# Attention's rounds dissolved into three strands, expert sums issued in four pieces, and the first unit of the last quarter taken ahead

## The chip, the core and the metric

One core of a Trainium2 chip runs the whole program. The core has five engines with their own instruction queues: TensorE (PE), VectorE (DVE), ScalarE (ACT), GpSimd (POOL) and SyncE (SP), which here only issues DMAs; GpSimd issues the indirect DMAs (gather and scatter). The metric is the device time of one execution in microseconds, as the median of several runs.

## The reference

The input x has 16 sequences of 512 rows with 256 channels, in fp32. Four layers follow each other, each added to its input after a layer norm:

```
x = x + gated_deltanet(layernorm(x))      # a recurrence over the 512 rows, 16 heads of 16
x = x + moe(layernorm(x))                 # 16 experts, 4 a row, and a shared one
x = x + attention(layernorm(x))           # causal, 16 heads of 16, rmsnorm and rope on q and k
x = x + moe(layernorm(x))                 # the same weights as above

# deltanet, one row t:                     # moe:
S = S + beta * outer(v - S k, k)           scores = sigmoid(x @ gate_w.T)
o = S q                                    idx = top_k(scores + gate_b, 4)
                                           w = 2.5 * scores[idx] / sum(scores[idx])
# attention:                               y = sum_e w_e * (silu(x @ w1_e.T) * (x @ w3_e.T)) @ w2_e.T
p = softmax(q k.T / 4 + causal)            y = y + shared expert
out = (p v) @ Wo
```

## The kernel before

**One list of stages.** `stages()` (line 127) makes one list, `order`, of named stages such as `step`, `w_dot` or `y_sum`, and each engine then walks the whole list and issues what is its own in each stage. So the order on every engine's queue is the order of that list, and an instruction that waits holds all behind it on its engine. The list is woven from generators ("strands"): every `yield` ends a step and gives a cost, `step()` advances a strand by one step, and `run(credit)` advances it while its credit lasts. `misc` is the pool of seven PSUM banks; the eighth, bank 6, collects the product with V.

**Units and groups.** A unit is 512 rows. Units 0 to 15 are the rows of the first moe (unit 4q + n: quarter q of the sequences 4n to 4n + 3), units 16 to 31 those of the second (unit 16 + b: sequence b). A unit has four rows of work J of 128 rows each, J = 4 * unit ... + 3. `GROUPS = [4, 4, 4, 1, 3, 2, 4, 4, 4, 2]` units form groups, which are routed together: three groups cover units 0 to 11, then unit 12 alone, units 13 to 15, 16 and 17, 18 to 21, 22 to 25, 26 to 29, and 30 and 31. For each group the strand `heads()` computes layer norm, gate and shared expert (`head`), the positions (`route`), and scatters each J with four indirect DMAs into an expert-sorted buffer (`x_row`: GpSimd scales the row, `x_move`: four scatters). For J from 64 to 119 it then yields SPACE more times. The strand `tiles()` works through 16 tiles a unit and 16 more a group: 256 KB of weights and 128 KB of rows in, 128 KB out. The strand `sums()` gathers for each J its four expert rows (`y_in`: four indirect DMAs on GpSimd into a ring of five tiles) and accumulates them on VectorE (`y_sum`, line 1371). Routing of a group waits in the list until the sums of the group two before it are in.

**The recurrence.** VectorE runs the 512 steps in four quarters of 128 (`step`, lines 1084 to 1100, in three thirds). After every third `heads` gets the credit HEAD_RATE, `tiles` TILE_RATE, `sums` SUM_RATE and the projection of the next quarter PROJECT_RATE. Operations of a step are tied in a chain: products with k and with q (L1084, L1086), their reductions (L1089, L1092), the difference (L1094), its outer product (L1097), the new state (L1100).

**The turnover.** After the last quarter the state's outputs are transposed (`u_turn`), `first_rows` projects them for units 12 to 15, all four side by side, while tiles and sums step along but heads does not. Then `second_setup` loads the constants of attention by DMA and GpSimd prepares them (lines 1620 to 1632), and only then heads may go on to unit 12. `prepare(0)` advances all strands until the sum of J = 48 is in the list, since sequence 0 needs it.

**Attention.** For each of 16 sequences (batches) `attention(b)` yields turns with a phase: 1 for projection, norm, rope and the split of q and k (32 turns), 2 and 3 for the scores, 4 for the output projection (12 turns). After each turn `tiles` gets PHASE_RATE[phase]; `heads` steps every second turn, `sums` every fourth. The heads form four groups of four. For each group `largest(hg)` issues eleven stages of scores (`m_dot`, L899) with VectorE's row maxima (`m_max`, L1202), then splits the maxima into three bf16 parts, transposes them (`m_part`, `m_turn`, `m_out`). `weigh(hg)` issues for four key tiles of 128 and four heads the scores again with the maximum subtracted by a second matmul (`w_dot`, L916 and L918), the exponential on ScalarE (`w_exp`, L1516), the causal select of the diagonal 128 x 128 on GpSimd (L1650), and the product with V (`w_pv`, L930), which waits for the select and stands about four turns behind its scores; at the end `w_out` copies bank 6. The rounds: round 0 is `largest(0)`, round r has `weigh(r - 1)` beside `largest(r)`, round 4 is `weigh(3)` alone, and a round ends when both are done.

Of the kernel before, what the change touches and what calls it, by code (L numbers as in the profile page):

```python
# [15 lines left out]
NQ = SEQ // 128  # L16
# [100 lines left out]
def stages():  # L117
# [129 lines left out]
    def attention(b, norm):  # L247
# [62 lines left out]
        def largest(hg):  # L310
            k = 4 * b + hg
            pend, l = None, 11 * k
            for qt in range(NQ):
                nh = {0: 4, 1: 2, 2: 1, 3: 1}[qt]
                for h0 in range(4 * hg, 4 * hg + 4, nh):
                    mi, mf = yield from misc.take()
                    put("m_dot", b, qt, h0, nh, mi, mf)
                    if pend:
                        put("m_max", *pend)
                        misc.give(pend[-1], "mx", pend[1] + 1)  # L320
                    pend = (b, l, qt, h0, nh, mi)
                    l += 1
                    yield
            put("m_max", *pend)
            misc.give(pend[-1], "mx", pend[1] + 1)
# [9 lines left out]
            yield  # L335

        def weigh(hg):
            k = 4 * b + hg
            pend = None
            for kt in range(NQ):  # L340
                for a in range(4):
                    w = 16 * k + 4 * kt + a
                    mi, mf = yield from misc.take()
                    put("w_dot", k, kt, a, mi, mf)
                    if pend:
                        put("w_exp", *pend)
                        misc.give(pend[-1], "we", w)
                    pend = (k, kt, a, mi)
                    if a == 3 and kt:
                        put("w_pv", k, kt - 1)  # L350
                    yield
            put("w_exp", *pend)
            misc.give(pend[-1], "we", 16 * k + 16)
# [1489 lines left out]
```

## Time and profile before

| | |
|---|---|
| three runs | 5775.86, 5779.35, 5791.94 us, median 5779.35 |
| profiled execution | 5783.49 us, span 5782.3 us, mean granted TensorE clock 0.799 |
| busy over the span | PE 3420.9 (59%), DVE 4123.7 (71%), ACT 1976.3 (34%), POOL 1764.7 (31%) |
| chain that ended last | DVE 41%, PE 30%, issue 11%, POOL 9%, ACT 4%, DMA 3% |
| HBM | 378.89 MB read, 209.72 MB written, 102 GB/s over the span |

The shares over the whole span are means over stages of different kind, so they say little by themselves; the windows among the rows below give the stages apart. The profiled execution's own time is its span and 1.2 us around it.

### The profile page before, as it was taken

How to read it: one execution, taken by the hardware profiler on the slowest of the kernel's cores; microseconds unless marked ns; L12 is line 12 of the kernel's file. 1: busy time of each engine (PE TensorE's matmuls, PEld its weight loads, DVE VectorE, ACT ScalarE, POOL GpSimd, SP SyncE). 2: the span in 40 equal slices, each digit the busy share in tenths (PEclk: the TensorE clock that was granted, in tenths of full speed). 3: DMA queues.
4: the chain of work that ended last, by engine and by line, in shares of the span. 5: the costliest groups of instructions: out<-in, count | busy, mean ns of one | idle time of the engine just before them, and what ended most of it. 6: DMA issues, size and time to landing. Idle time of an engine off the chain costs nothing.

```text
span 5782.3 us, 71376 instructions
## 1 busy us (share of the span) xinstructions
PE 3420.9 (59%) x20276; PEld 2403.0 (42%) x20372; DVE 4123.7 (71%) x10439; ACT 1976.3 (34%) x4743; POOL 1764.7 (31%) x2760
## 2 busy tenths in 40 slices
PE   6312053663436533263548878876788778877664
PEld 3101031452315422152435555543565555545554
DVE  1999989999899988998356656665566556654333
ACT  3111021231213311031236545644555545544232
POOL 1010014303461133403352233235211433244523
PEclk8655576796668866697779999987999989988887
DMA  1210001462215421363532334311233323333776
GB/s 48 114 40 7 0 20 48 136 173 67 67 57 172 140 64 55 113 189 114 154 110 75 99 121 126 95 54 65 79 90 90 115 89 117 113 99 121 244 226 200
DMA packets 429265, 593.40 MB, mean 103 GB/s; under 512 B 57680, under 2 KB 304080, under 8 KB 428752
## 3 DMA queue, kind: packets, MB, share of 16 engines
q1 hardware_dynamic: 379728, 454.55, 26.3%
q0 software_dynamic: 49152, 134.28, 7.0%
q8 instruction: 173, 2.83, 0.2%
q14 instruction: 212, 1.74, 0.1%
HBM read 378.89 MB, written 209.72 MB: 102 GB/s over the span
## 4 chain that ended last, share of the span: by engine, by line
DVE 41%; PE 30%; issue 11%; POOL 9%; ACT 4%; DMA 3%; SPq 2%; another core or an unknown queue 1%; DVEq 0%; ACTq 0%; POOLq 0%
PE psum L1020 5%; DVE rec L1084 5%; DVE rec L1086 4%; DVE skb L1089 4%; DVE rec L1097 4%; DVE rec L1100 4%; POOL xbuck L1669 4%; DVE region L1092 3%; PE psum L930 3%; PE psum L878 3%; PE psum L1028 3%; DVE psum L1202 2%; DVE acc L1371 2%; POOL yg L1679 2%; PE psum L918 2%
## 5 line engine op out<-in xcount | busy, mean ns | idle before, releaser
L1020 PE MATMUL psum<-xgT,w 128*128 128x128 f32 x5376 | 798.9, 296 | 105.1 <-issue 57.9
L1679 POOL DMA_INDIRECT yg<-ybuck,words x512 | 529.6, 1034 | 988.1 <-issue 641.2
L1020 PEld LDWEIGHTS psum<-xgT,w 128*128 128x128 f32 x5376 | 729.2, 209 | 160.2 <-issue 123.2
L1028 PE MATMUL psum<-w_w2T,hid 128*128 x1344 | 475.0, 438 | 360.1 <-DVE hid L1353 227.0
L1202 DVE CUSTOM_DVE_ANT_0 psum<-psum,xo 128x128 f32<-128x128 f32 (+3 forms) x1024 | 473.7, 520 | 224.5 <-PE psum L899 204.5
L1669 POOL DMA_INDIRECT xbuck<-srow,words x512 | 521.9, 1019 | 152.3 <-issue 128.9
L810 PE MATMUL psum<-w_ident,xn 128*128 128x128 f32 x512 | 105.8, 343 | 773.5 <-ACT xn L1388 767.8
L1516 ACT ACTIVATE region<-psum 128x512 f32<-128x512 f32 (+3 forms) x1024 | 412.0, 443 | 348.4 <-PE psum L918 313.7
L1551 ACT ACTIVATE xgT<-psum 128x256 f32<-128x256 f32 x672 | 257.1, 383 | 760.7 <-PE psum L1010 709.2
L1650 POOL TENSOR_SCALAR_AFFINE_SELECT region<-region 128x128 f32<-128x128 f32 x1024 | 288.8, 300 | 670.5 <-ACT region L1516 656.2
L1038 DVE SCALAR_TENSOR_TENSOR sil<-sil,psum 128x128 f32<-128x128 f32 (+1 forms) x472 | 139.4, 295 | 448.9 <-ACT sil L1560 366.2
L1371 DVE SCALAR_TENSOR_TENSOR acc<-yg,words,acc 128x256 f32<-128x256 f32 x512 | 254.4, 497 | 233.5 <-DMA yg<-ybuck,words 87.4
L810 PEld LDWEIGHTS psum<-w_ident,xn 128*128 128x128 f32 x512 | 73.7, 174 | 803.1 <-ACT xn L1388 746.0
L1028 PEld LDWEIGHTS psum<-w_w2T,hid 128*128 128x128 f32 x1344 | 223.4, 205 | 440.0 <-issue 436.0
L1010 PE MATMUL psum<-w_ident,xg 128*128 128x128 f32 x1344 | 280.1, 294 | 170.3 <-DMA xg<-xbuck 162.6
L1097 DVE TENSOR_TENSOR rec<-ub,region 128x512 f32<-128x512 f32 x512 | 370.8, 724 | 12.5
L1084 DVE TENSOR_TENSOR rec<-rec,region 128x512 f32<-128x512 f32 x512 | 362.3, 708 | 12.5
L1100 DVE TENSOR_TENSOR rec<-rec 128x512 f32<-128x512 f32 x512 | 358.4, 700 | 11.8
L1086 DVE TENSOR_TENSOR rec<-rec,region 128x512 f32<-128x512 f32 x508 | 357.9, 704 | 0.0
L1585 POOL TENSOR_SCALAR small<-small 128x4 f32<-128x4 f32 (+1 forms) x80 | 30.3, 379 | 1060.9 <-DVE small L1051 1058.1
L930 PE MATMUL psum<-region 128*32 128x512 f32 (+3 forms) x2048 | 278.5, 468 | 121.4 <-POOL region L1650 96.9
L1089 DVE TENSOR_REDUCE skb<-rec 128x32 f32<-128x512 f32 x512 | 347.4, 678 | 0.1
(201 smaller groups left out, 7576.4 us busy)
## 6 DMA issues: line engine op xcount, KB each, us to landing
w<-in_w13T SPq DMA_DIRECT2D x672, 256.0 KB
xg<-xbuck SPq DMA_DIRECT2D x672, 128.0 KB
ybuck<-yrow SPq DMA_DIRECT2D x672, 128.0 KB
xbuck<-x SPq DMA_DIRECT2D x40, 512.0 KB, 5.3
x_scratch<-res SPq DMA_DIRECT2D x64, 256.0 KB
acc<-x_scratch SPq DMA_DIRECT2D x128, 128.0 KB
xbuck<-srow,words POOLq DMA_INDIRECT x512
yg<-ybuck,words POOLq DMA_INDIRECT x512
```

Source lines behind the costliest of these rows:

```text
L930: o = e.matmul(psum[32 * a:32 * a + 32, 6, kt * 128:SEQ], vb[:, kt, k % 4 * 4 + a, :], P[w % 8][:, 0:n], start=(kt == 0), stop=(kt == NQ - ...
L1020: o = e.matmul(psum[:, mi, half], w13[I % 3][:, k, half], xgT[I % 2][:, k, :], start=(k == 0), stop=(k == 1), skip_group_check=True)
L1028: o = e.matmul(psum[:, mi, 0:D], hid[hi][:, 0:128], w2T[:, bass.ds(expert.pop(I), 1), :].rearrange("p a b -> p (a b)"), start=True, stop=True)
L1084: e.tensor_tensor(tk[:, :, :, :], S[:, :, :, :], ktt, ALU.mult).then_inc(s["scan"], 1)
L1086: e.tensor_tensor(tq[:, :, :, :], S[:, :, :, :], bc(kq[:, :, t - 1, 16:32], 2, 16), ALU.mult).then_inc(s["scan"], 1)
L1089: e.tensor_reduce(skb[:, :, :], tk[:, :, :, :], AX.X, ALU.add).then_inc(s["scan"], 1)
L1097: e.tensor_tensor(tk[:, :, :, :], bc(ub[:, :, :], 3, 16), ktt, ALU.mult).then_inc(s["scan"], 1)
L1100: e.tensor_tensor(S[:, :, :, :], S[:, :, :, :], tk[:, :, :, :], ALU.add).then_inc(s["scan"], 1)
L1202: o = e.tensor_tensor_reduce(scores, scores, maskw[:, SEQ - n:SEQ], -1.0, BIG, ALU.add, ALU.min, mx[:, qt, h0 + i:h0 + i + 1])
L1516: e.activation(P[w % 8][:, 0:n], psum[:, mi, 0:n], ACT.Exp, scale=HD ** -0.5).then_inc(s["we"], 1)
L1669: e.indirect_dma_start(xbuck[g % 2], bass.IndirectOffsetOnAxis(ap=posu[g % 2][:, J - ROWS0[g], k:k + 1], axis=0), srow[J % 2], None).then_ ...
L1679: e.indirect_dma_start(yg[y % 5], None, ybuck[g % 2][0:TILES_OF[g] * 128, :], bass.IndirectOffsetOnAxis(ap=posu[g % 2][:, J - ROWS0[g], k: ...
```

## The change

The list of stages is woven differently; no arithmetic changes.

- In attention the rounds are gone. One strand issues the maxima of the head groups one after the other (group 2 and 3 wait until the weights of the group two before are issued). When a group's maxima are issued, its small chain (parts, transpose, copy) starts as a strand of its own. One strand issues the weights, each group as soon as its chain is out, and the last V product with its copy becomes a strand of its own. A turn steps all of them and has phase 3 once the first chain is out, before that phase 2.
- `y_sum` is issued as four stages; for J below 48 the strand yields between them. SUM_RATE goes from 0.2 to 0.35.
- SPACE goes from 4 to 2, PHASE_RATE[3] from 0.04 to 0.06.
- After the last quarter the rows of unit 12 go first; then `heads` may start on it while the rows of units 13 to 15 are issued. A head waits in the list for its own unit's rows. GpSimd's preparation of the constants moves behind the scatter of unit 12's group, as `second_fill`.

```diff
-HEAD_RATE, TILE_RATE, SUM_RATE, PROJECT_RATE = 0.6, 0.5, 0.2, 0.15
-SCATTER, SPACE = 1.3, 4
-PHASE_RATE = {LIGHT: 0.32, 1: 0.32, 2: 0.2, 3: 0.04, 4: 0.3}
+HEAD_RATE, TILE_RATE, SUM_RATE, PROJECT_RATE = 0.6, 0.5, 0.35, 0.15
+SCATTER, SPACE = 1.3, 2
+PHASE_RATE = {LIGHT: 0.32, 1: 0.32, 2: 0.2, 3: 0.06, 4: 0.3}
...
-        def largest(hg):
+        turning, closing, out, weighed = [], [], set(), set()
+
+        def largest():
+            for hg in range(4):
+                while hg >= 2 and hg - 2 not in weighed:
+                    yield
...                                   # m_dot and m_max as before
+                turning.append(Strand(turn(hg)))
+
+        def turn(hg):
...                                   # m_part, m_turn, m_out as before
+            out.add(hg)
+
+        def weigh():
+            for hg in range(4):
+                while hg not in out:
+                    yield
...                                   # w_dot, w_exp and three w_pv as before
+                weighed.add(hg)
+                closing.append(Strand(close(hg)))
+
+        def close(hg):
             k = 4 * b + hg
             yield
             yield
             put("w_pv", k, NQ - 1)
             yield
             put("w_out", k)
-        for hg in range(5):
-            both = [Strand(weigh(hg - 1))] if hg else []
-            both += [Strand(largest(hg))] if hg < 4 else []
-            while not all(t.done for t in both):
-                for t in both:
-                    t.step()
-                yield 2 if hg == 0 else 3
+        heads_of, weights = Strand(largest()), Strand(weigh())
+        while not (heads_of.done and weights.done and all(t.done for t in closing)):
+            for t in closing + [weights] + turning + [heads_of]:
+                t.step()
+            yield 3 if out else 2
...                                   # heads()
+                while b < NB and b not in added:
+                    yield LIGHT
                 yield from head(b)
...
             filled.add(g)
+            if UNIT0[g + 1] == NB - 3:
+                put("second_fill")
...                                   # sums()
-                put("y_sum", g, J)
+                for k in range(4):
+                    put("y_sum", g, J, k)
+                    if J < 48 and k < 3:
+                        yield LIGHT
...                                   # after the last quarter
     rows = [Strand(first_rows(NQ - 1, n)) for n in range(4)]
+    while not rows[0].done:
+        for t in rows[0:1] + streams[1:]:
+            t.step()
+    turned.add(NQ - 1)
     while not all(t.done for t in rows):
-        for t in rows + streams[1:]:
+        for t in streams + rows:
             t.step()
     put("second_setup")
-    turned.add(NQ - 1)
```

## Rows read from the trace of the kernel before

**Rows 1.** The page's busy tenths in 40 slices of 144.6 us.
```profile
PE   6312053663436533263548878876788778877664
...
DVE  1999989999899988998356656665566556654333
```

**Rows 2.** Windows: length, busy us of PE, PEld, DVE, ACT, POOL; clock, DMA, GB/s.
```profile
159.00:2699.00 2540.00, 1029.87 (x4902) 738.00 (x4902) 2374.61 (x4692) 503.40 (x1260) 613.77 (x654) 0.70 0.28 86
2699.00:2941.00 242.00, 128.07 (x748) 110.84 (x748) 99.53 (x335) 58.42 (x162) 98.73 (x137) 0.74 0.47 143
2941.00:5305.00 2364.00, 1860.18 (x12622) 1254.89 (x12719) 1454.59 (x4851) 1222.88 (x2803) 821.82 (x1709) 0.90 0.31 95
```

**Rows 3.** Waits of TensorE, 2941 to 5305: us in total, times, longest.
```profile
PE psum L930 <- POOL region L1650: 96.9, 43, 8.1
...
PE psum L916 <- DVE region L1202: 29.3, 23, 8.0
```

**Rows 4.** Windows of batches 5 and 6, L1028 alone (two matmul records a tile).
```profile
3667.00:3796.00 129.00, 13.85 (x42) 6.83 (x42) 0.97 0.31 92
3796.00:3962.00 166.00, 1.88 (x6) 1.06 (x6) 0.79 0.20 64
```

**Rows 5.** Windows of the rounds and the last round: batch 5, then batch 6.
```profile
3735.00:3770.00 35.00, 32.43 (x248) 16.23 (x251) 27.41 (x120) 23.87 (x59) 14.00 (x47) 1.00 0.16 47
3770.00:3784.00 14.00, 13.26 (x114) 7.46 (x113) 1.43 (x7) 10.21 (x31) 5.82 (x21) 1.00 0.13 39
...
3858.00:3918.00 60.00, 39.49 (x250) 17.95 (x252) 41.00 (x167) 22.05 (x50) 33.09 (x62) 0.77 0.22 68
3918.00:3949.00 31.00, 18.92 (x107) 8.38 (x107) 6.65 (x19) 10.22 (x28) 25.92 (x48) 0.86 0.31 100
```

**Rows 6.** Timeline of VectorE in a step with a sum: start, length, operation.
```profile
1433.23 2.25 DVE L1371 SCALAR_TENSOR_TENSOR acc<-yg,words,acc 128x256 f32<-128x256 f32 x4
1435.39 0.69 DVE L1097 TENSOR_TENSOR rec<-ub,region 128x512 f32<-128x512 f32 x1
```

**Rows 7.** Timeline of VectorE in a step without one.
```profile
1445.65 0.68 DVE L1092 TENSOR_REDUCE region<-rec 128x32 f32<-128x512 f32 x1
1446.24 0.18 DVE L1094 TENSOR_TENSOR ub<-region,skb 128x32 f32<-128x32 f32 x1
1446.45 0.69 DVE L1097 TENSOR_TENSOR rec<-ub,region 128x512 f32<-128x512 f32 x1
```

**Rows 8.** Window of the recurrence, L1371 alone: busy us (instructions).
```profile
159.00:2699.00 2540.00, 69.42 (x144) 0.70 0.28 86
```

**Rows 9.** The chain in order of time: the load of batch 0.
```profile
2927.02 3.80 DMA xnT<-x_scratch
```

**Rows 10.** Timeline of GpSimd in the turnover: setup, a gather, first scattered row.
```profile
2741.43 0.19 POOL L1623 CAST w_attn<-w_attn 128x4 bf16<-128x4 f32 x1 [3.06 <-DMA w_attn<-in_sel]
...
2746.29 1.01 POOL L1679 DMA_INDIRECT yg<-ybuck,words  x1 [0.16 <-issue]
...
2793.40 0.78 POOL L1659 TENSOR_SCALAR srow<-x,stq 128x256 f32<-128x256 f32 x1 [5.93 <-DVE words L1336]
```

**Rows 11.** Window of the 32 tiles of unit 12, L1028 alone.
```profile
2833.00:2913.00 80.00, 20.32 (x64) 10.33 (x64) 0.99 0.70 203
```

**Rows 12.** Windows with L1028 alone: no tiles, and the tail.
```profile
3811.00:4116.00 305.00, 0.00 (x0) 0.00 (x0) 0.80 0.19 62
...
5305.00:5568.00 263.00, 59.43 (x168) 28.30 (x168) 0.86 0.77 231
```

**Rows 13.** Timelines of GpSimd and TensorE around a burst of scatters.
```profile
3914.02 1.07 POOL L1669 DMA_INDIRECT xbuck<-srow,words  x1 [0.16 <-issue]
...
3919.15 1.06 POOL L1650 TENSOR_SCALAR_AFFINE_SELECT region<-region 128x128 f32<-128x128 f32 x4
...
3919.51 1.33 PE L930 MATMUL psum<-region 128*32 128x384 f32 x6 [0.44 <-issue]
```

**Rows 14.** Window of the scattered rows of units 18 to 21, L1659 alone.
```profile
3892.00:4080.00 188.00, 9.41 (x16) 0.80 0.18 63
```

More of the change, by code:

```diff
@@ L308, in attention @@
             yield 1
-        def largest(hg):
-            k = 4 * b + hg
[L312 to L325, printed above, removed]
+        turning, closing, out, weighed = [], [], set(), set()
[3 more added lines that the diff above has]
+                    yield
+                k = 4 * b + hg
+                pend, l = None, 11 * k
+                for qt in range(NQ):
+                    nh = {0: 4, 1: 2, 2: 1, 3: 1}[qt]
+                    for h0 in range(4 * hg, 4 * hg + 4, nh):
+                        mi, mf = yield from misc.take()
+                        put("m_dot", b, qt, h0, nh, mi, mf)
+                        if pend:
+                            put("m_max", *pend)
+                            misc.give(pend[-1], "mx", pend[1] + 1)
+                        pend = (b, l, qt, h0, nh, mi)
+                        l += 1
+                        yield
+                put("m_max", *pend)
+                misc.give(pend[-1], "mx", pend[1] + 1)
+                turning.append(Strand(turn(hg)))
+        def turn(hg):
+            k = 4 * b + hg
             for i in range(3):
@@ L335, in largest @@
             yield
-        def weigh(hg):
-            k = 4 * b + hg
[L339 to L353, printed above, removed]
+            out.add(hg)
+        def weigh():
+            for hg in range(4):
+                while hg not in out:
+                    yield
+                k = 4 * b + hg
+                pend = None
+                for kt in range(NQ):
+                    for a in range(4):
+                        w = 16 * k + 4 * kt + a
+                        mi, mf = yield from misc.take()
+                        put("w_dot", k, kt, a, mi, mf)
+                        if pend:
+                            put("w_exp", *pend)
+                            misc.give(pend[-1], "we", w)
+                        pend = (k, kt, a, mi)
+                        if a == 3 and kt:
+                            put("w_pv", k, kt - 1)
+                        yield
+                put("w_exp", *pend)
+                misc.give(pend[-1], "we", 16 * k + 16)
+                weighed.add(hg)
+                closing.append(Strand(close(hg)))
+        def close(hg):
+            k = 4 * b + hg
             yield
@@ L1361, in vector @@
             elif name == "y_sum":
-                g, J = u
-                a, j = acc[J % 2], J - ROWS0[g]
+                g, J, k = u
+                a, j, y = acc[J % 2], J - ROWS0[g], 4 * J + k
                 dv.wait_ge(s[f"ai{J % 2}"], 16 * (J // 2) + 16)
                 dv.wait_ge(s["rv"], RV0[g + 1])
-                for k in range(4):
-                    y = 4 * J + k
-                    dv.wait_ge(s[f"yg{y % 5}"], 16 * (y // 5) + 16)
-                    if k:
-                        dv.wait_ge(s["ysum"], y)
-                    e.scalar_tensor_tensor(a, yg[y % 5], ck[g % 2][:, j, k:k + 1], a, ALU.mult,
-                                           ALU.add).then_inc(s["ysum"], 1)
+                dv.wait_ge(s[f"yg{y % 5}"], 16 * (y // 5) + 16)
+                if k:
+                    dv.wait_ge(s["ysum"], y)
+                e.scalar_tensor_tensor(a, yg[y % 5], ck[g % 2][:, j, k:k + 1], a, ALU.mult,
+                                       ALU.add).then_inc(s["ysum"], 1)
     def scalar():
@@ L1619, in gpsimd @@
                 e.tensor_tensor(xo[oi], xo[oi], boA[:, :], ALU.add).then_inc(s["rb"], 1)
-            elif name == "second_setup":
+            elif name == "second_fill":
                 po.wait_ge(s["oadd"], 64)
@@ L1774, in sync @@
             elif name == "y_sum":
-                g, J = u
-                sp.wait_ge(s["ysum"], 4 * J + 4)
-                e.dma_start(of_half(J, out_rows), acc[J % 2]).then_inc(s[f"ao{J % 2}"], 16)
+                g, J, k = u
+                if k == 3:
+                    sp.wait_ge(s["ysum"], 4 * J + 4)
+                    e.dma_start(of_half(J, out_rows), acc[J % 2]).then_inc(s[f"ao{J % 2}"], 16)
             elif name == "end":
```

## The prediction

> **What bounds the kernel now.** First the busy tenths, to see that the run has two halves: in slices 2 to 19 of 40 VectorE stands at 8 or 9 tenths, in slices 22 to 37 TensorE at 6 to 8 [rows 1]. Windows put numbers to them [rows 2]: the recurrence, 159 to 2699 us (VectorE busy 2375 of 2540); a turnover, 2699 to 2941, in which no engine is over 53% busy; attention, 2941 to 5305 (TensorE 1860 of 2364, DMA share 0.31). Then comes a tail to the end of the span, 5782, whose first 263 us move 231 GB/s at DMA share 0.77 [rows 12]. Then the waits of TensorE within attention: the longest is the product with V waiting for GpSimd's causal select, 97 us in 43 waits, and 29 us go to banks that VectorE's maxima hold [rows 3]. Last, a batch without row traffic beside one with it: 129 us with 21 tiles against 166 with 3 [rows 4], and their phases, where the difference lies [rows 5].
>
> **The change part by part.**
>
> *Sums in four stages.* In the recurrence the four accumulations of a row are one block, 2.16 us from its start to the start of the next multiply (1433.23 to 1435.39), 0.54 each [rows 6], since each waits for the one before. Step operations without such a tie start 0.59 apart for 0.68 of work, so they overlap by 0.09; a tied pair (ub, then the multiply by it) starts 0.21 apart for 0.18, so it doesn't [rows 7]. A piece put between a tied pair fills such a place. Apart, I take a piece at 0.45 instead of 0.54, which gives 0.36 a row, and another 0.14 for tied pairs that were empty: 0.5 a row. The recurrence has 144 accumulations, 36 rows [rows 8]: 18 us off, on the engine that sets the end there. Bounds: 0 (each piece keeps 0.54) and 36 x 0.9 = 32 (0.40 a piece, and three tied pairs each 0.1 better). The pace stays: 4 steps of the strand at rate 0.2 and 7 at 0.35 both give a row in 7 thirds of a step.
>
> The Trainium skill (VectorE: DVE Perf Modes, "The DRAIN you can't avoid") speaks against this: a chain of operations with a semaphore after each took as long there as one with a single semaphore at the end. By it these 18 us would be 0. The trace does not agree as far as it goes: tied operations start later after their predecessor's end than untied ones, by 0.12 us [rows 7]. It stands below as a rival.
>
> *The turnover.* Unit 12 gates it: its first rows, head, routing, 4 scattered rows, 32 tiles and first sum, after which batch 0's load ends the chain's wait at 2931 [rows 9]. Today the rows of all four units go first, then the setup, for whose constants GpSimd waits 3.1 us and on which it then works until its next gather, 2741.4 to 2746.3 [rows 10]. From there to unit 12's first scattered row, 2793.4, GpSimd's queue holds 28 gathers of sums, 1.3 us apart [rows 10]. Three gains: the setup leaves the chain, 8 us; three quarters of the row work no longer stand ahead of the head, though they still share the engines with it, 10 us; and a row of sums takes 7 steps of its strand instead of 4, so that some 10 gathers fewer precede the scatter, 12 us. Late next is the tile pass: the sums put off run beside it, some 8 rows of 0.79 MB (six transfers of 128 KB), 6 MB on top of the 16 MB that its 80 us at 203 GB/s move [rows 11]. Were 231 GB/s [rows 12] the ceiling, it would last 17 us longer; I take 5. So 25 us off; bounds 0 and 50.
>
> *Attention without rounds.* Counted in the loops: today 18 turns of maxima alone, then four rounds of 20, 98 of the 143 turns of a batch. New: the maxima of groups 0 and 1 run on (turns 1 to 22), group 0's weights start at 20, group 1's at 36 with group 2's maxima, group 2's at 55, group 3's at 71, and the last close ends at 91: 136 turns a batch. The instructions are the same. In the quiet batch TensorE is busy 32.4 of 35 us in the rounds and 13.3 of 14 in the last one [rows 5]: at most some 4 us can go, and 1.2 more tiles (0.06 x 73 turns for 0.04 x 80) want half of it. In the busy batch the same phases take 91 us, 58.4 of them busy [rows 5]. There a select sits behind a burst of four scatters, 3914.0 to 3919.15, and the product that needs it starts at 3919.51 [rows 13]. What changes is the last product of a group: three turns of the next group's dots now stand ahead of it in TensorE's queue, so that they are issued while it would wait; behind it the bank of the sum is copied by ScalarE, and the next group's first product, four turns later, waits for that copy. The other three products have the lead they had. Of the 97 + 29 us [rows 3] I count a quarter, that product's share, as gone: 31. Six come back: of a batch's turns some 42 now have weights without maxima (31 before), in which a lead of four turns is shorter. 25 us off over 16 batches. Bounds: 90 off (most of the 126) and 40 on.
>
> *Two pauses for four.* A scattered row of units 16 to 29 takes 12 turns now (row, move, four pauses, the strand stepping every second turn) and 8 then. 16 rows lie within 188 us [rows 14]; they would take 125. The bursts are as many as before; that they come closer can make GpSimd the bound, and is the slow rival.
>
> *Earlier groups, higher rate.* No tile runs from 3811 to 4116 [rows 12], since units 18 to 21 are scattered only by 4080 [rows 14]. They would be ready 62 us sooner, and a batch takes 22 tiles, not 21. Carried through the turns: that group ends in batch 11, units 22 to 25 end in the middle of batch 15, and units 26 to 29 are scattered by turn 100 of it instead of 120, so that some 4 of their tiles, beside the 4 left over today, and 5 rows of sums get in before attention ends. I count 8 tiles (0.52 MB: weights 256 KB, in and out 128 KB each) and 5 rows of sums out of the tail: 8.1 MB, at 231 GB/s 35 us, 36 with a shorter restart. In attention the 8 tiles cost 25 us at most, at the tail's pace of 84 tiles in 263 us [rows 12]; half or more fall where TensorE idles: 10 on. Bounds of the tail: 0 and 60 off.
>
> **Sum.** -18 - 25 - 25 + 10 - 36 = -94. The profiled execution took 5783.5 us (span 5782.3); the median of the runs, 5779.35, is 4 lower. 5783.5 - 94 - 4 = 5685.
>
> **Rivals.**
> 1. Attention and tail give nothing: the added tiles cost in attention what they save behind it, and the stalls only move. For: TensorE is 79% busy there. Against: 33 us of the busy batch's 91 are idle [rows 5]. Then 18 + 25 off: 5736.
> 2. Slower: GpSimd becomes the bound of attention. Its burst with the scaled row is 5.6 us, and 8 turns hold 8 selects of 0.3: 8.0 us of work, in turns of weights alone that last 14 us for 20 [rows 5], 5.6 for 8. If each of the 56 closer rows costs 2.5 us more than today, 140 are added: 5825. It decides from 94 / 56 = 1.7 us a row. For: the 97 us of waits for the select. Against: a row costs GpSimd the same work as now, and 12 turns at 0.7 us are hardly longer than it even today.
> 3. Both kinds of stall go (the bound of 90): 5620.
> 4. The four stages save nothing, the rest holds, as the skill's rule would have it: 5703.
> 5. The last large group does not come forward: forced advances and the wait for the sums two groups back keep it behind 5305. Then +10 and -36 fall away: 5711.
>
> **Chances.** Forecast 0.42, rival 1 0.20, rival 2 0.14, rival 3 0.12, rivals 4 and 5 0.06 each. About 0.3%, 17 us, is what a measurement can tell from no change. Rival 2 lies above that, a third of rival 1, with its own spread, within it: faster 0.79, same 0.07, slower 0.14. The range for 8 in 10 leaves out most of rival 2 and the lower part of rival 3: 5600 to 5780. The forecast's own is 5640 to 5725.
>
> **What would show it.** Right: the accumulations of the recurrence singly among step operations, and its stretch some 18 us shorter; unit 12's first scattered row within 60 us of the recurrence's end, and batch 0 some 25 us earlier; tiles of units 26 to 29 before attention ends; the wait of the V product for the select under 80 us; a tail near 440. Wrong: attention as long as its 2364 us, the select's wait above 100 us (then rival 2), or a turnover that keeps its 242 us.

## The result and the profile after

Four executions of the changed kernel took 5710.86 to 5734.44 us, median 5720.71; four of the kernel before on the same chip 5773.94 to 5791.94, median 5777.60. The ratio is 0.9894 [0.9874, 0.9914]: 1.1% faster, 57 us by the medians, where 94 were forecast. The time lies within the range (5600 to 5780) and just inside the forecast's own (5640 to 5725). The profiled execution took 5734.44 us, the slowest of its four; that of the kernel before took 5783.49.

The page of the changed kernel (span; busy us of each engine; busy tenths in 40 slices), against [rows 1]:

```profile
span 5733.2 us, 71459 instructions
PE 3423.1 (60%) x20279; PEld 2404.4 (42%) x20372; DVE 4101.4 (72%) x10439; ACT 1958.1 (34%) x4743; POOL 1769.6 (31%) x2760
PE   6312054573536634163558878875888787877664
DVE  1999988999899988998456646665667466745333
```

The work is the same and the outline too. The windows of the three stretches of [rows 2], and the tail:

```profile
159.00:2683.00 2524.00, 1041.46 (x4902) 746.90 (x4902) 2359.31 (x4691) 504.06 (x1260) 617.40 (x653) 0.70 0.28 87
2683.00:2917.00 234.00, 122.45 (x748) 106.72 (x748) 97.50 (x336) 57.75 (x162) 97.90 (x136) 0.75 0.50 149
2917.00:5272.00 2355.00, 1868.02 (x12714) 1259.87 (x12808) 1463.19 (x4894) 1211.23 (x2820) 841.36 (x1728) 0.90 0.32 98
5272.00:5733.00 461.00, 285.58 (x1597) 238.95 (x1596) 155.67 (x466) 128.23 (x391) 179.79 (x192) 0.79 0.72 215
```

There are four small gains and no large one: 2540 to 2524, 242 to 234, 2364 to 2355, and the tail. With the ends taken to a tenth (first step operation, end of the operation behind the last step, first projection of batch 0, last output projection, end of the span):

| us, profiled executions | before | after | difference | forecast |
|---|---|---|---|---|
| recurrence | 2539.0 | 2523.8 | -15 | -18 |
| turnover | 242.7 | 234.5 | -8 | -25 |
| attention | 2364.1 | 2354.3 | -10 | -25 + 10 |
| tail | 477.0 | 461.3 | -16 | -36 |

They sum to -49, the difference of the two profiled executions. Within attention (each batch cut at TensorE's first projection, first scores of the maxima, first scores of the weights and first transpose of the output, summed over 16): preparation 833 to 863, maxima alone 238 to 289, weights with maxima 1063 to 972, output 230 and 230. Maxima and weights together lost 40 us, and the preparation gave 30 back.

**Sums.** VectorE of the changed kernel in a step of the recurrence with a row of sums (start, length, operation), against [rows 6, 7]:

```profile
1431.04 0.18 DVE L1122 TENSOR_TENSOR ub<-region,skb 128x32 f32<-128x32 f32 x1
1431.14 0.48 DVE L1397 SCALAR_TENSOR_TENSOR acc<-yg,words,acc 128x256 f32<-128x256 f32 x1
1431.54 0.68 DVE L1125 TENSOR_TENSOR rec<-ub,region 128x512 f32<-128x512 f32 x1
...
1433.49 0.47 DVE L1397 SCALAR_TENSOR_TENSOR acc<-yg,words,acc 128x256 f32<-128x256 f32 x1
1433.89 0.69 DVE L1128 TENSOR_TENSOR rec<-rec 128x512 f32<-128x512 f32 x1
```

From a piece to the step's next operation it is 0.40 us each time (1431.14 to 1431.54, 1433.49 to 1433.89), where a piece of the block took 0.54. That 0.54 is a mean of two kinds: the block ends at 1435.48 and its last piece lasts 0.48, so it began at 1435.00 and gave way after 0.39, and the three before it, which the next one waits for, took 0.59 each [rows 6]. The first piece here stands between the tied pair, which is 0.50 long with it and 0.21 without [rows 7], so this one costs 0.29.

**Turnover.** GpSimd of the changed kernel: unit 12's first scattered row, the start of the setup, the gather behind it. Then waits from 2778 to 2815 (us, times, longest) and, in a block of its own, the like wait of the kernel before, from 2811 to 2840. Then pieces of the chain of the changed kernel (start, us, what):

```profile
2755.78 0.56 POOL L1685 TENSOR_SCALAR srow<-x,stq 128x256 f32<-128x256 f32 x1 [1.29 <-DVE words L1364]
...
2784.05 0.20 POOL L1649 CAST w_attn<-w_attn 128x4 bf16<-128x4 f32 x1
...
2788.74 1.03 POOL L1705 DMA_INDIRECT yg<-ybuck,words  x1 [0.16 <-issue]
```
```profile
ACT xn L1410 <- POOL small L1618: 50.9, 1, 50.9
...
PE psum L838 <- ACT xn L1414: 41.7, 1, 41.7
```
```profile
PE psum L810 <- ACT xn L1388: 29.3, 2, 27.6
```
```profile
2793.96 1.06 POOL small L1614
...
2805.90 1.71 PE psum L1048 x8
...
2903.53 3.73 DMA xnT<-x_scratch
```

The scatter begins 73 us behind the recurrence's end (2755.8 against 2683.1), before 95 us (2793.4 against 2698.5) [rows 10]; 22 us are won there. But 14 of them are lost again before the first down product, which comes 126 us behind that end (2809.5) where it came 135 behind it (2833.2): unit 13's head needs a small operation of GpSimd (2794.0), which stands behind the setup and a gather, and its transposes stand in TensorE's queue ahead of the first tile. TensorE waits 41.7 us for them, and the first tile comes only at 2805.9. The same head stood before the first tile in the kernel before, where the wait was 27.6 us; it is longer now by the 14 that are lost.

**Attention.** Waits of TensorE, 2917 to 5270 (us, times, longest), against [rows 3], and in a block of its own a row of the kernel before that [rows 3] leaves out; then windows of batches 5 and 6 with the down product's line alone, against [rows 4]:

```profile
PE psum L958 <- POOL region L1676: 57.0, 27, 7.3
...
PE psum L958 <- issue: 36.8, 19, 6.3
...
PE psum L944 <- DVE region L1230: 15.1, 21, 2.4
```
```profile
PE psum L930 <- issue: 24.0, 17, 4.4
```
```profile
3654.00:3783.00 129.00, 14.96 (x44) 7.27 (x44) 0.97 0.29 86
3783.00:3951.00 168.00, 0.00 (x0) 0.00 (x0) 0.76 0.20 64
```

L958 is the product with V (L930 before), L944 the weights' scores (L916 before). The row of the select fell from 96.9 to 57.0, but the same product's row "issue", a wait that the profile puts down to nothing, rose from 24.0 to 36.8. Together they are 120.9 and 93.8: the product stands 27 us less, not 40. The wait for the maxima fell from 29.3 to 15.1. The quiet batch does 22 tiles in the time in which it did 21; the busy one takes 168 us instead of 166, with none instead of 3.

**Tail.** Windows with that line alone: the last 80 us of attention, then the tail's tile pass over units 26 to 29, against [rows 12]:

```profile
5192.00:5272.00 80.00, 0.87 (x2) 0.15 (x1) 0.89 0.27 83
5272.00:5522.00 250.00, 60.99 (x159) 28.72 (x160) 0.83 0.74 218
```

80 us of attention stand nearly without a tile. The tail's pass has 80 tiles, where it had 84. Its sums (L1397) are 148, where the kernel before has 160 from 5305 on.

### The profile page after: what moved, and what is told of

Its sections match the earlier page's. It is cut to its first block, busy times and chain, and to the rows that moved or that the text cites. A ratio compares the mean times of both kernels' runs of the same rounds, so it can differ in the third digit from the quotient of the medians.

```text
span 5733.2 us, 71459 instructions
## 1 busy us (share of the span) xinstructions
PE 3423.1 (60%) x20279; PEld 2404.4 (42%) x20372; DVE 4101.4 (72%) x10439; ACT 1958.1 (34%) x4743; POOL 1769.6 (31%) x2760
## 4 chain that ended last, share of the span: by engine, by line
DVE 42%; PE 31%; issue 12%; POOL 7%; ACT 4%; DMA 3%; SPq 1%; another core or an unknown queue 1%; DVEq 0%; ACTq 0%; POOLq 0%
PE psum L1048 5%; DVE rec L1112 5%; DVE rec L1114 4%; DVE skb L1117 4%; DVE rec L1125 4%; DVE rec L1128 4%; DVE region L1120 3%; DVE psum L1230 3%; PE psum L958 3%; PE psum L906 3%; PE psum L1056 3%; POOL xbuck L1695 2%; DVE acc L1397 2%; PE psum L944 2%; PE psum L946 2%
## 5 line engine op out<-in xcount | busy, mean ns | idle before, releaser
L1397 DVE SCALAR_TENSOR_TENSOR acc<-yg,words,acc 128x256 f32<-128x256 f32 x512 | 252.7, 494 | 264.4 <-DMA yg<-ybuck,words 120.9
L1120 DVE TENSOR_REDUCE region<-rec 128x32 f32<-128x512 f32 x508 | 343.0, 675 | 0.0
```

Of the source, the lines that this page charges most:

```text
L1120: e.tensor_reduce(vo[:, :, t - 1, :], tq[:, :, :, :], AX.X, ALU.add).then_inc(s["scan"], 1)
```

## The experiments

Each kernel was timed beside the kernel before on the same chip. The chips are numbered here by the order of the runs; the record does not name that of the result, and its time suggests a fourth. The kernel before itself took 5777.60 (chip 1, the result above), 5716.60 (chip 2), 5766.16 (chip 3) and 5720.85 us (chip 4). So the ratios are compared, not the times. Of the stretches, only those of one pair of chips are set against each other: 1 with 3, and 2 with 4. On chips 2 and 4 three kernels whose attention is unchanged (e1, e4, h2) serve as "attention and tail before": 2326 to 2331 and 450 to 454 us, and likewise two kernels with the turnover as before (e2, e3 on chip 2): 240 us. The phases of attention are cut as above.

### Chip 2: the four parts, each alone

**e1_sums**

```diff
-HEAD_RATE, TILE_RATE, SUM_RATE, PROJECT_RATE = 0.6, 0.5, 0.2, 0.15
+HEAD_RATE, TILE_RATE, SUM_RATE, PROJECT_RATE = 0.6, 0.5, 0.35, 0.15
...
-                put("y_sum", g, J)
+                for k in range(4):
+                    put("y_sum", g, J, k)
+                    if J < 48 and k < 3:
+                        yield LIGHT
```

> The kernel before with only the sums in four stages (and their rate 0.35). Theory: the recurrence ends 15 to 16 us earlier, as in the whole change (2698.5 to 2682.8), since the accumulations stand singly among step operations; the turnover changes by at most 5 us, so the time falls by 12 to 20 us. Rival (the order of the sums is free, as a semaphore in a chain costs nothing): the recurrence keeps its end within 3 us and the time stays; the 15 us of the whole change would then come from elsewhere.

Measured 5696.02 us, 0.9959 [0.9945, 0.9973]. Its recurrence:

```profile
155.00:2679.00 2524.00, 1040.92 (x4902) 744.55 (x4902) 2359.55 (x4690) 504.21 (x1260) 618.37 (x654) 0.70 0.28 87
```

The recurrence lasts 2524 us, as in the whole change, and VectorE's busy time is 2360 where it was 2375 [rows 2]. All traces agree: with the sums in four stages 2510 to 2524 us, without them 2539 to 2550. By chip the four stages are worth 15 us (chip 1), 17 to 26 (chip 2) and 25 to 31 (chip 4); the same recurrence took 2510 to 2523 us in four kernels of chip 3, so a single trace tells it to some 10 us. The theory holds, and the rival is out. Unit 12's first scattered row comes 82 us behind the recurrence's end, 11 earlier than in e2 and e3, but the first down product is 132 us behind that end, as there (132 and 134), and the turnover is 239: the earlier scatter alone brings 1 us.

**e2_strands**

```diff
-        for hg in range(5):
...
+        heads_of, weights = Strand(largest()), Strand(weigh())
+        while not (heads_of.done and weights.done and all(t.done for t in closing)):
...
```

> The kernel before with only attention's rounds dissolved into strands (four pauses, rate 0.04). Theory: the scores phases of the 16 batches lose some 40 us in sum, the wait of the V product for the select falls from 97 us to 60 to 70, projection phases keep their 837 us, and the time falls by 25 to 45 us. Rival (fewer turns only shift work: 7 turns fewer a batch give the tiles, scatters and sums less of attention): the attention gets 30 us shorter but the tail longer by as much, and the time stays within 10 us.

Measured 5693.88 us, 0.9956 [0.9942, 0.997]. Its tail and attention; then its wait for the select and that of e1 on the same chip:

```profile
5230.00:5694.00 464.00, 297.61 (x1763) 253.96 (x1761) 175.19 (x530) 141.97 (x431) 199.28 (x218) 0.82 0.78 233
```
```profile
2944.00:5230.00 2286.00, 1826.79 (x12643) 1222.23 (x12642) 1442.85 (x4829) 1197.15 (x2781) 814.11 (x1703) 0.91 0.32 97
```
```profile
PE psum L946 <- POOL region L1666: 112.7, 56, 11.4
```
```profile
PE psum L933 <- POOL region L1651: 125.4, 60, 13.6
```

Attention is 2286 us, 43 less than in the kernels of these chips with rounds, and the tail 464, 13 more: with 7 turns fewer a batch 261 tiles are done in attention instead of 268. The gain in time is 0.44%, 23 us by the medians, just under the 25 to 45 of the expectation; the phases of scores lost 39 us, near its 40. The wait for the select fell by 13 us, from 125.4 in e1 to 112.7, and not to the 60 to 70 that were expected from the 97 of chip 1: that row is 125 us in the kernels with rounds of chips 2 and 4. A fall of 13 under a gain of 43 also says that the row does not measure the strands; what it leaves out is read under f6.

**e3_scatter**

```diff
-SCATTER, SPACE = 1.3, 4
-PHASE_RATE = {LIGHT: 0.32, 1: 0.32, 2: 0.2, 3: 0.04, 4: 0.3}
+SCATTER, SPACE = 1.3, 2
+PHASE_RATE = {LIGHT: 0.32, 1: 0.32, 2: 0.2, 3: 0.06, 4: 0.3}
```

> The kernel before with only two pauses for four and the rate 0.06 for 0.04. Theory: units 26 to 29 are scattered some 60 us earlier and a few sums leave the tail, but the closer bursts cost some 10 us in each projection phase that they fall into, so that the sum is small: 0 to 15 us off. Rival 1 (the forecast's): the tail gets 36 us shorter and attention 10 longer, 26 off. Rival 2: GpSimd bounds attention, 20 or more on.

Measured 5726.47 us, 1.0013 [1.0002, 1.0025]. Its attention and tail:

```profile
2949.00:5298.00 2349.00, 1868.69 (x12817) 1267.26 (x12818) 1472.24 (x4904) 1224.65 (x2822) 845.55 (x1736) 0.90 0.32 99
5298.00:5726.00 428.00, 270.33 (x1588) 230.29 (x1586) 151.28 (x456) 127.55 (x389) 171.94 (x184) 0.82 0.76 227
```

Here the tail falls by 24 us and attention grows by 20. The growth lies in the rounds (1063 us in e1, 1085 here): batches 2, 6, 10, 11 and 14 take 50 us more there, and batches 3, 7, 8 and 13 take 39 less. With rounds, what is moved forward costs as much as it saves. The time is 0.13% longer, where 0 to 15 us off were expected.

**e4_first**

```diff
+    while not rows[0].done:
+        for t in rows[0:1] + streams[1:]:
+            t.step()
+    turned.add(NQ - 1)
...
+            if UNIT0[g + 1] == NB - 3:
+                put("second_fill")
```

> The kernel before with only unit 12 ahead and the constants' preparation behind its scatter. Theory: unit 12's first scattered row comes 15 to 25 us earlier, but the head of unit 13, queued on GpSimd behind the preparation, holds TensorE's queue and with it the first tile, so that batch 0 begins only 5 to 12 us earlier: 5 to 12 us off. Rival (the gain of the scattered row is passed on whole): 20 to 25 off.

Measured 5729.49 us, 1.0022 [1.0013, 1.0032]. Its turnover:

```profile
2698.00:2952.00 254.00, 128.34 (x748) 110.26 (x748) 101.17 (x336) 58.07 (x162) 98.49 (x137) 0.73 0.45 137
```

Alone this part is a loss: the turnover is 254 us, 14 longer than the 240 of e2 and e3, where the expectation and its rival both had it shorter. The first scattered row itself comes late, 100 us behind the recurrence's end where it comes 93 and 94 behind it in e2 and e3.

### Chip 3: the whole again, and two variants of it

**a1_after_again**: the changed kernel without an edit, so there is no diff.

> The whole change, unedited, as a control. Its parts alone gave -0.41% (sums), -0.44% (strands), +0.13% (scatter and rate) and +0.22% (first unit ahead), -0.50% in sum, where the whole change gave -1.06%. Theory (the parts need each other: unit 12 ahead pays only when a row of sums takes seven steps, so that fewer gathers stand before its scatter): again 0.9875 to 0.991, with batch 0 some 234 us after the recurrence's end. Rival (additive, the difference is one of chips): about 0.995.

Measured 5692.87 us, 0.9878 [0.9864, 0.9892]: 1.2% faster.

```profile
2910.00:5231.00 2321.00, 1857.03 (x12806) 1244.80 (x12807) 1462.28 (x4894) 1210.42 (x2820) 842.36 (x1729) 0.91 0.33 100
5231.00:5684.00 453.00, 281.09 (x1598) 236.77 (x1596) 155.84 (x466) 127.58 (x391) 179.28 (x192) 0.80 0.74 218
```

**g1_sums_strands**: the sums and the strands, with neither the pauses and the rate nor unit 12 ahead. Against the changed kernel:

```diff
-SCATTER, SPACE = 1.3, 2
-PHASE_RATE = {LIGHT: 0.32, 1: 0.32, 2: 0.2, 3: 0.06, 4: 0.3}
+SCATTER, SPACE = 1.3, 4
+PHASE_RATE = {LIGHT: 0.32, 1: 0.32, 2: 0.2, 3: 0.04, 4: 0.3}
...
-    while not rows[0].done:
```

> The kernel before with the two parts that gained alone, the sums in four stages and attention's strands; four pauses, rate 0.04, all four units' rows first. Theory: they add up, one in the recurrence and one in attention, -0.85%, 48 us off; the whole change is then better than this by its turnover, 8 us. Rival (the other two parts are plain losses): this beats the whole change.

Measured 5737.28 us, 0.9944 [0.993, 0.9959].

```profile
2920.00:5263.00 2343.00, 1859.33 (x12642) 1237.99 (x12642) 1443.72 (x4829) 1199.37 (x2781) 815.64 (x1702) 0.90 0.31 95
5263.00:5745.00 482.00, 295.45 (x1761) 249.23 (x1760) 174.75 (x530) 142.07 (x430) 199.78 (x218) 0.84 0.75 225
```

So the pauses, the rate and unit 12 ahead, each of no use alone, take another 0.66% off (0.9878 / 0.9944): 22 us of attention, 29 of the tail, 7 of the turnover in the traces. These are more than the 44 us between the medians, since g1's profiled execution is its slowest and a1's its fastest. The theory for g1 was the plain sum of the two parts, -0.85%; it gives -0.56%.

**f3_space4**

```diff
-SCATTER, SPACE = 1.3, 2
+SCATTER, SPACE = 1.3, 4
```

> The whole change with four pauses again instead of two, all else kept (rate 0.06). Theory: closer bursts cost attention about what they bring the tail: within 8 us of the whole change, attention 15 to 25 us shorter (its rounds and projections in batches 10, 11, 14 and 15), the tail 15 to 20 longer. Rival of the forecast (earlier groups pay 36 us for 10): 20 us or more longer than the whole change.

Measured 5710.13 us, 0.991 [0.9896, 0.9923]. Its tail:

```profile
5228.00:5704.00 476.00, 286.50 (x1650) 241.03 (x1650) 167.28 (x509) 132.63 (x402) 198.60 (x218) 0.81 0.74 219
```

Two pauses for four are worth 0.32% in the whole, 17 us by the medians, and they lie in the tail: 476 us here, 453 with two, at an attention of 2325 and 2321. Both have 128 tiles in the tail. What leaves it with two pauses is 3 rows of sums (12 of the 43 operations by which VectorE's 509 become 466) and the start of the pass over units 26 to 29. The expectation had the two within 8 us, with a shorter attention here; neither holds.

**f4_both**: a pass over tiles goes at the fast rate until its ninth slot, and the setup of attention's constants stands in unit 12's pass.

```diff
+            starting.add(g)
             for i in range(n + 8):
+                if i == 8:
+                    starting.discard(g)
+                if UNIT0[g + 1] == NB - 3 and i == 16:
+                    put("second_fill")
...
-            streams[1].run(PHASE_RATE[phase])
+            streams[1].run(max(PHASE_RATE[phase], 0.32) if starting else PHASE_RATE[phase])
```

> The whole change with two more edits: while the first eight slots of a group's tile pass fill, the strand gets rate 0.32 in every phase, and the constants' preparation is issued at slot 16 of unit 12's tile pass. Theory (the tail did not shorten as forecast, since from the first load to the first down product a pass needs seven slots, at 0.06 a turn most of a batch): the first tile of units 26 to 29 is done before attention ends, in the list at turn 101 of batch 15, the tail gets 15 to 30 us shorter, batch 0 begins 5 to 9 us earlier, and the whole is 15 to 35 us faster than the whole change. Rival (tiles in attention cost there what they save): within 8 us of it.

Measured 5684.41 us, 0.9862 [0.9847, 0.9876], the fastest of all, though its interval overlaps that of the whole change (8 us by the medians).

```profile
2898.00:5254.00 2356.00, 1861.30 (x12882) 1253.23 (x12882) 1471.07 (x4918) 1213.66 (x2838) 847.06 (x1739) 0.91 0.33 100
5254.00:5682.00 428.00, 255.72 (x1521) 215.43 (x1520) 146.70 (x441) 122.03 (x373) 167.94 (x181) 0.82 0.74 219
```

Now the last large group does come forward (277 tiles within attention instead of 272), and the tail is 428 us, 26 less. But attention is 2356, 35 more, in the one profiled execution that each has: 12 in batch 0, and 8, 16 and 9 in batches 7, 11 and 15, in which a pass starts, against 11 less in the others. The medians, which hold both, differ by 8, so that the rival (within 8 us) fits and the expected 15 to 35 do not. The setup moved out of the way brought 3 us of turnover (234.7 to 232.0), and TensorE's wait for unit 13's head is 37.4 us instead of 41.9.

### Chip 4: two pairs, and the select left out

**h1_strands_scatter**: strands, two pauses and the rate of 0.06, on the kernel before.

```diff
-SCATTER, SPACE = 1.3, 4
+SCATTER, SPACE = 1.3, 2
...
+        heads_of, weights = Strand(largest()), Strand(weigh())
```

> The kernel before with attention's strands, two pauses and rate 0.06, without the other two parts. Alone the strands gave -0.44% and the scatter and rate +0.13%; in the whole change, without them, -0.5% was missing beyond what the turnover explains. Theory (strands and pace need each other: 7 turns fewer a batch give the tiles, scatters and sums less of attention, which two pauses and the higher rate give back): -0.6 to -0.8%, the tail 20 us shorter than with strands alone. Rival (additive): -0.3%.

Measured 5653.61 us, 0.989 [0.9874, 0.9905].

```profile
2935.00:5213.00 2278.00, 1840.49 (x12811) 1237.91 (x12810) 1462.58 (x4894) 1208.23 (x2820) 846.00 (x1729) 0.92 0.33 102
5213.00:5647.00 434.00, 273.47 (x1596) 231.81 (x1594) 155.24 (x466) 128.30 (x391) 179.15 (x192) 0.81 0.76 228
```

Against the kernels of these chips with rounds, attention is some 50 us shorter and the tail some 17. The closer rows, which cost the rounds 22 us (e3), cost the strands nothing: their weights take 967 us, with four pauses and the lower rate 980 (e2). The ratio to e2 is 0.9934, as was that of a1 to g1. It is a gain of 1.1%, more than the 0.6 to 0.8% expected.

**h2_sums_first**: the sums in four stages and unit 12 ahead.

```diff
+                for k in range(4):
+                    put("y_sum", g, J, k)
...
+    while not rows[0].done:
```

> The kernel before with the sums in four stages and unit 12 ahead. Alone -0.41% and +0.22%. Theory (a row of sums of seven steps lets fewer gathers stand before unit 12's scatter, which is what makes it pay): the turnover takes 232 to 235 us, from the end of the recurrence to batch 0, where the sums alone had 239 and unit 12 ahead alone 254; -0.5 to -0.6%. Rival (additive): 250 us and -0.2%.

Measured 5681.19 us, 0.993 [0.9917, 0.9944].

```profile
2671.00:2905.00 234.00, 122.80 (x747) 107.12 (x748) 96.44 (x336) 57.88 (x161) 97.43 (x136) 0.75 0.49 149
```

The turnover is the whole change's. Unit 12 ahead takes 254 us alone and 235 with the slower sums, which alone give 239: it pays only with them, and then by 4 us in the traces. The whole gain, 0.70%, is a little above the 0.5 to 0.6 expected.

**f6_nosel_before** and **f5_nosel_after**: the kernel before and the changed one without the causal select. What they leave out is the zeroing of the diagonal tiles' upper half; all later stages take the unmasked weights.

```diff
-                    pe.wait_ge(s["causal"], w + 1)
+                    pe.wait_ge(s["we"], w + 1)
...
-                e.affine_select(P[w % 8][:, 0:128], P[w % 8][:, 0:128], pattern=[[1, 128]], compare_op=ALU.is_ge,
-                                fill=0.0, base=0, channel_multiplier=-1).then_inc(s["causal"], 1)
```

> The kernel before with the causal select on GpSimd left out: the product with V waits for the exponential, so that the diagonal tiles of the weights stay unmasked. Theory (the rounds lose their time to selects that stand behind bursts of indirect DMAs, 97 us of waits and what the clock adds): the rounds of the 16 batches, 1039 us, lose 100 to 160, most in batches 2, 3, 6, 7, 10, 11, 14 and 15. Rival (TensorE's own work bounds them): under 50.

> The whole change with the causal select left out in the same way. Theory (the strands gained by hiding part of these waits): it gains 40 to 60 us less from it than the kernel before does. Rival (the strands gained by filling the boundaries of the rounds, not by hiding selects): it gains as much.

Measured 5509.17 us, 0.9638 [0.9624, 0.9653], and 5479.67 us, 0.9586 [0.9571, 0.9601]. Attention of the one and of the other:

```profile
2935.00:5048.00 2113.00, 1738.71 (x12725) 1191.85 (x12724) 1445.56 (x4852) 1215.87 (x2803) 539.34 (x686) 0.93 0.35 107
```
```profile
2900.00:5038.00 2138.00, 1778.58 (x12811) 1211.16 (x12810) 1452.53 (x4894) 1205.80 (x2820) 556.25 (x705) 0.92 0.35 108
```

With rounds the select costs 218 us of attention (2330 in h2, 2112 here), more than the 100 to 160 of the expectation, while TensorE's wait for it is 125 us in h2. The rest is found in the product with V, taken apart by its form. Its four stages are 512, 384, 256 and 128 columns wide, one for each key tile. For each of them, busy us and mean ns, then the idle time before it: h2 (rounds, L940), then h1 (strands, L946), then f6, where all of them together are busy 198.78 us and wait for nothing:

```profile
L940 PE MATMUL psum<-region 128*32 128x512 f32 x512 | 94.5, 658 | 30.0 <-POOL region L1658 29.8
L940 PE MATMUL psum<-region 128*32 128x384 f32 x512 | 62.7, 499 | 7.9 <-POOL region L1658 7.9
L940 PE MATMUL psum<-region 128*32 128x256 f32 x512 | 67.7, 415 | 45.5 <-POOL region L1658 45.2
L940 PE MATMUL psum<-region 128*32 128x128 f32 x512 | 65.3, 321 | 42.1 <-POOL region L1658 42.1
```
```profile
L946 PE MATMUL psum<-region 128*32 128x512 f32 x512 | 78.1, 621 | 17.3 <-POOL region L1666 17.3
L946 PE MATMUL psum<-region 128*32 128x384 f32 x512 | 71.6, 523 | 25.0 <-POOL region L1666 25.0
L946 PE MATMUL psum<-region 128*32 128x256 f32 x512 | 52.4, 404 | 17.3 <-POOL region L1666 17.3
L946 PE MATMUL psum<-region 128*32 128x128 f32 x512 | 49.4, 300 | 39.7 <-POOL region L1666 39.7
```
```profile
2935.00:5048.00 2113.00, 198.78 (x2048) 48.53 (x2048) 0.93 0.35 107
```

| us on chip 4, busy and idle before | 512 | 384 | 256 | 128 | all |
|---|---|---|---|---|---|
| rounds (h2) | 124 | 71 | 113 | 107 | 405 |
| strands (h1) | 95 | 97 | 70 | 89 | 349 |
| rounds, no select (f6) | 73 | 55 | 43 | 32 | 199 |

The stages overlap by up to 10 us, so they sum to more than the whole. Of the 218 us, 206 lie in the product with V: 125 are its idle rows, and 81 stand inside its busy time, 280 us with selects and 199 without. A stage is four products that wait for four selects, one after the other. Without selects 512 records of 0.64 us fill 73.4 us, so about four run side by side; held apart by selects of 0.3 us they still overlap, but fill 94.5, and no row of waits shows the difference. The rest of TensorE's work is some 40 us shorter too, at a granted clock of 0.93 instead of 0.90, and other waits grow by 28.

Without selects the strands are worth nothing: maxima and weights together take 1090 us in rounds (f6) and 1106 in strands (f5, with 4 tiles more in attention), with selects 1303 (h2) and 1251 (h1). By the ratios the changed kernel gains 31 to 40 us less from the missing select than the kernel before, where 40 to 60 were expected, and the rival, as much, is out. This shows what the strands do: they lay the next group's scores over the wait for the select. They hide some 50 us of it, 57 in the product with V alone; in the changed kernel the select still costs the weights about 140 (967 to 824).

## Why the prediction was right and wrong

**Sums, -18: right, -15** (15 to 31 over all traces). The mechanism is the forecast's, a block of tied operations taken apart. A piece costs 0.40, the favourable bound, not 0.45. By the rows 3 pieces of 36 blocks give 0.19 each, 21 us, and some 3 more come from the pieces between a tied pair. Rival 4, the rule that a semaphore in a chain costs nothing, falls by e1: 0.41% from this alone. The trace does not agree with the rule (the Trainium skill, VectorE: DVE Perf Modes, "The DRAIN you can't avoid") for these operations: 0.59 us with the wait, 0.40 without it.

**Turnover, -25: mis-sized, -8.** The step that failed is "the setup leaves the chain, 8 us; three quarters of the row work no longer stand ahead of the head, though they still share the engines with it, 10 us". The setup did not leave the chain: it is put behind unit 12's scatter, where unit 13's head waits on GpSimd behind it, and TensorE's queue brings that wait before unit 12's first tile. I followed what stands ahead of the scatter and not what stands between it and the tiles. The trace before had it already: there TensorE stood 27.6 us for the same head before the first tile, so an earlier scatter could bring little. The sign "first scattered row within 60 us" failed too, with 73. The third gain, fewer gathers ahead through slower sums, came in size for the scatter (e1: 11 us where I had 12), but alone it shortened the turnover by 1 us. Still it is what makes unit 12 ahead pay: without it (e4) the turnover is 14 us longer than in e2 and e3. That the work put ahead then shares GpSimd with the gathers is the likely reason and was not tested. f4 moves the setup and takes 3 to 4 us off, so the setup is not the larger part; the head of unit 13 in front of the tiles is, by the waits of the trace, but no run took it away. On chip 4 the turnover of h2 is only 2 to 3 us shorter than in f6 and h1, on chips 1 and 3 the gain is 7 to 8.

**Attention, -25 + 10 = -15: -10, close by luck of two errors.** Maxima and weights gained 39 to 50 us where I had 25, and on chip 1 the preparation took 30 back where I had 10 for tiles. For the first, the kind of gain was right (the next group's dots are issued while the product would wait) and two steps under it were wrong. The quarter "Of the 97 + 29 us" took the row for the whole wait, of which it holds 125 of 206 us on chip 4. And "What changes is the last product of a group", "The other three products have the lead they had" is not what the stages show: the last one gains 18 us, the third 43, the first 29, and the second loses 26. On chip 1, by the same rows, it is 21, 40, 22 and a loss of 22. Why the third gains most stays open. The sign "under 80 us" came true with 57 on chip 1, but with the "issue" row it is 94, and e2 and h1 have 112.7 and 99.3.

The preparation's 30 us on chip 1 lie in batches 11 (14) and 15 (8) above all, where scatters stand close on GpSimd. In batch 11's, VectorE stands up to 5.0 and 7.3 us and TensorE 7.5 us at a time in rows of "issue", which name no cause. On chip 3 the same batches are long in a1 (62 and 61 us), less so with four pauses (f3: 53 and 57). On chips 2 and 4 the same closer rows left the whole preparation at 819 (e3) and 815 us (h1), where it is 818 to 819 without them. What this is stays open.

**Tail, -36: the largest miss, -16.** The step that failed is "some 4 of their tiles, beside the 4 left over today, and 5 rows of sums get in before attention ends". The 4 left over did get in, and 3 rows of sums: 4.5 MB, by my own price of 231 GB/s 19 us. So the price held and the count failed. None of the last large group's did, though its rows were scattered in turn 68 of batch 15, earlier than the 100 I had, and its first load stands in turn 83. A pass puts seven slots of loads and first products before its first down product, and phase 3 gives 0.06 of a slot a turn, so that attention ends at turn 136 before the eighth; I counted turns up to the scatter and none for that start. To this extent rival 5 was right: the term belonged to it. f4 takes the start away, the 5 tiles come forward and the tail falls to 428 us, but attention takes the gain back. So there my term was also wrong in kind: of 26 us saved in the tail, some 8 are left in the time. I had priced a tile in attention at 1.25 us (10 for 8), and TensorE is 79% busy there. But f4 speeds the start of every pass, and only 9 of its 35 us lie in the last batch; what the last group's tiles alone would cost was not run.

**Rivals.** Rival 1 (5736) foresaw the exchange between attention and tail, but with rounds, where e3 shows it; with strands the pair takes another 0.66% off. Rival 2, GpSimd as the bound, exists in small: 22 us over 56 rows in e3's rounds, 0.4 a row, where it needed 1.7. Rival 3 (all stalls of the select and maxima gone) was too small a bound: without the select 218 us go.

**The parts do not add.** Alone they sum to -0.50% (-0.41, -0.44, +0.13, +0.22), the whole gives -1.06 and -1.22. The two pairs sum to -1.80%, more than the whole, but they were measured on chip 4 and the whole on chips 1 and 3. Whether the whole would reach it there was not run and stays open. All four terms came out below the forecast in the profiled executions, so none covered for another, and the time lies within the forecast's own range because that is 85 us wide.

## What to carry to other kernels

A wait's row tells how long one engine stood idle, not what its cause is worth: add the "issue" row of the same instruction, look how long its busy time is without the cause, and leave the cause out in one run (here the row says 125 us, the run 218). Compare such rows on one chip: for the same attention this one is 97 us on chip 1, with 24 more under "issue", and 125 on chips 2 and 4, with none there. When work is moved forward in a woven order, follow it to its first product through every queue: the pipeline's start and the neighbour's head ate most of both moves. And test parts in pairs: closer scatters and unit 12 ahead each lost alone, and each paid beside another part, the scatters clearly (with the strands), unit 12 by some 4 us (with the sums).

## What the runs showed of the hardware

An accumulation on VectorE (128x256, 0.48 us) that the next one waits for takes 0.59 us from start to start; where the next operation does not wait for it, 0.40; put between a tied pair, 0.29. A block of four tied ones takes 0.54 each on the mean. The product with V is busy 280 us in attention while it waits for selects and 199 us when it does not: here a busy row held 81 us of waiting. The same kernel took 5717 to 5778 us on these four chips, 1.1%, as much as this change is worth. The recurrence was alike (2539 to 2550 us unstaged); attention was 2364 us on chip 1 and 2326 to 2331 on chips 2 and 4, and the tail 477 and 450 to 454. The tail, at a DMA share of 0.72 to 0.78, ran at 215 to 225 GB/s in the windows of chips 1 and 3 and at 227 to 234 in those of chips 2 and 4.
